# Modulation stage reordered, and one image's group-norm statistics moved into the linear stage

## The reference, cut to what matters

```python
x = x + focal_modulation(_gn(x))     # L0: projection, three depthwise convolutions, modulator, layer norm, projection
x = x + fp8_linear_unit(_gn(x))      # L1: layer norm, 64->512 linear, relu(a)*b, 256->64 linear, both on fp8-rounded values
x = x + gated_scan(_gn(x))           # L2: circular 7x7 convolutions, scan of 8 steps, 64->64 linear
x = x + deform_conv(_gn(x))          # L3: offsets, bilinear gather of 9 taps, linear
def _gn(v, G=32, eps=1e-05):         # mean and variance over all positions and 2 channels
    g = v.reshape(B_, H_, W_, G, C_ // G)
    m = jnp.mean(g, axis=(1, 2, 4), keepdims=True); s = jnp.var(g, axis=(1, 2, 4), keepdims=True)
    return ((g - m) / jnp.sqrt(s + eps)).reshape(v.shape)
```

## Time and profile before

| | |
|---|---|
| median of three runs | 6727.5 us |
| the profiled execution's own time | 6720.4 us |
| its span, first to last instruction | 6718.6 us |
| granted TensorE clock, mean | 0.595 |
| stage C, start to the loads of stage L, groups 0 to 3 | 147.2, 210.3, 211.1, 221.0 us |
| stage L, from there to stage D, groups 0 to 3 | 294, 364, 367, 378 us |

### The profile page before, as it was taken

How to read it: one execution, slowest core, us unless ns; L and a number is a source line. 1 busy time by engine, 2 the same in 40 slices (tenths; PEclk the granted TensorE clock), 3 DMA queues, 4 the chain that set the end, 5 groups by cost and what they waited for, 6 DMA issues and landing times. The chain is left out here.

```text
span 6718.6 us, 66875 instructions
## 1 busy us (share of the span) xinstructions
PE 4037.8 (60%) x26416; PEld 3590.6 (53%) x26416; DVE 3327.1 (50%) x4118; ACT 1743.2 (26%) x3401; POOL 2877.0 (43%) x2617
## 2 busy tenths in 40 slices
PE   5864375678745576579644486667755465365333
PEld 4852275677633575468633385567643365364332
DVE  4357533534578544444478544353468734443332
ACT  2124234311233224321223234321223223022000
POOL 0000002534456544443455543544446645556676
PEclk9955555568555555558555555558655555555555
DMA  2830444458332844448423654439632474843332
GB/s 48 174 53 15 73 115 98 111 131 177 76 84 80 162 130 116 107 107 188 93 77 89 126 134 128 120 88 198 120 91 70 98 161 107 169 128 102 100 94 83
DMA packets 864530, 742.19 MB, mean 110 GB/s; under 512 B 667266, under 2 KB 744482, under 8 KB 860866
## 3 DMA queue, kind: packets, MB, share of 16 engines
q1 hardware_dynamic: 739802, 398.02, 29.9%
q0 software_dynamic: 124416, 339.90, 18.1%
HBM read 621.76 MB, written 117.51 MB: 110 GB/s over the span
## 5 line engine op out<-in xcount | busy, mean ns | idle before, releaser
L2067 POOL DMA_INDIRECT e_gb<-corner_table,e_idx x2592 | 2861.8, 1104 | 3820.5 <-DVE e_vw L2128 1842.4
L2128 DVE TENSOR_TENSOR e_vw<-e_gb,e_pc 128x1024 f32<-128x1024 f32 x576 | 756.4, 1348 | 500.4 <-DMA e_gb<-corner_table,e_idx 260.0
L2081 PE MATMUL e_pw<-wk,e_vt 128*128 128x64 f32 x2304 | 501.6, 391 | 614.8 <-ACT e_vt L2105 284.6
L2081 PEld LDWEIGHTS e_pw<-wk,e_vt 128*128 128x128 f32 x2304 | 471.7, 301 | 667.4 <-ACT e_vt L2105 400.2
L2094 PE MATMUL e_pv<-shifts,e_vw 128*128 128x128 f32 x2304 | 504.0, 392 | 169.4 <-DVE e_vw L2132 109.8
L2094 PEld LDWEIGHTS e_pv<-shifts,e_vw 128*128 128x128 f32 x2304 | 444.8, 222 | 175.1 <-DVE e_vw L2132 112.8
L492 PE MATMUL b_p<-b_x,b_tt 100*100 100x96 f32 x4096 | 423.7, 264 | 42.5 <-issue 42.5
L1467 PE MATMUL d_p<-d_wd,d_px 120*96 120x48 f32 x2048 | 345.4, 355 | 162.1 <-DMA d_px<-x_halo 86.4
L492 PEld LDWEIGHTS b_p<-b_x,b_tt 100*100 100x100 f32 x4096 | 410.4, 181 | 52.8 <-issue 51.7
L1467 PEld LDWEIGHTS d_p<-d_wd,d_px 120*96 120x96 f32 x2048 | 343.3, 258 | 167.7 <-DMA d_px<-x_halo 88.7
L2104 ACT ACTIVATE e_vt<-e_pv 128x512 f32<-128x512 f32 x288 | 171.0, 594 | 872.3 <-PE e_pw L2094 429.5
(11 more groups left out here) (306 smaller groups left out, 7623.5 us busy)
## 6 DMA issues: line engine op xcount, KB each, us to landing
b_tt<-zl SPq DMA_DIRECT2D x256, 234.0 KB
b_tt<-zl SPq DMA_DIRECT2D x128, 390.0 KB
e_gb<-corner_table,e_idx POOLq DMA_INDIRECT x2592
d_px<-x_halo SPq DMA_DIRECT2D x32, 1152.0 KB
corner_table<-f_xn SPq DMA_DIRECT2D x128, 288.0 KB
f_xall<-xpad SPq DMA_DIRECT2D x10, 2400.0 KB
d_wd<-zl SPq DMA_DIRECT2D x10, 1890.0 KB
x_halo<-d_xo SPq DMA_DIRECT2D x128, 144.0 KB
```

The source lines that it names most:

```text
L2067: nc.gpsimd.indirect_dma_start(self.gb[k][:, 4 * q:4 * q + 4, :].rearrange("p a c -> p (a c)"), None, T.table[m], off)\
L2081: nc.tensor.matmul(o, self.vt[:, q, :], T.wk[:, q, :], start=(q == 0), stop=False)
L2128: v.tensor_tensor(dst, self.gb[k][:, 4 * k0:4 * k1, :].rearrange("p (k a) c -> p k a c", a=4), bc(w, [128, k1 - k0, 4, C], 3), ALU.mult).t ...
```

## The change

In stage C the six products of p = 2 take another order, on PE and on DVE: one part of the older image, the three parts of the newer one, then the other two parts of the older one. The older image's scaled results go to a buffer of their own, `c_xm`, and their addition to `c_xs` comes after the newer image's variance. The statistics of the group's last image (image 3) leave stage C, whose groups i = 4 and 5 get shorter, and are taken in stage L: ACT squares after p = 0 of image 2, and the sums, the variance, the root and the scale come at p = 1 of image 2. The planned lengths of both stages change with it.

```diff
@@ class StageC
-    STEPS = [2, 8, 8, 4] + [8, 9, 12, 8] * (NI - 1) + [8, 1, 7, 6] + [6, 2, 1, 1]
+    STEPS = [2, 8, 8, 4] + [8, 9, 12, 8] * (NI - 1) + [8, 2, 7, 1] + [1] * 4
+        self.xm = sb("xm", [PP, NR, C])
...
+    @staticmethod
+    def bank_of(k, second, g):
+        base = 0 if k == 0 else 3 + 6 * (k - 1)
+        if k == NI:
+            return base + g
+        if second:
+            return base if g == 0 else base + 3 + g
+        return base + g + (k > 0)
@@ StageC.pe
-        if k >= 2 and p == 0:
+        if 2 <= k <= NI and p == 0:
             gn.pe_sum_wide(pe, self.psn, gn.use(G, 1, k - 2))
...
         if 1 <= k <= NI and p == 2:
-            for g in range(3):
...
+            back(0)
         if k < NI and p == 2:
             pe.wait_ge(S.c_gwr, NI * G + k + 1)
             for g in range(3):
...
+                forth(g)
+        if 1 <= k <= NI and p == 2:
+            back(1)
+            back(2)
@@ StageC.act
-        if 1 <= k <= NI and p == 3:
+        if 1 <= k < NI and p == 3:
             act.wait_ge(S.c_x1, NI * G + k)
             gn.act_square(act, self.xs[:, (k - 1) % 2, :, :], self.sq[:, :, :], gn.use(G, 1, k - 1))
@@ StageC.dve
+        if old:
+            back(0)
+        if new:
             dve.wait_ge(q_in[u], 80 * G + 16 + 32 * (k // 2 + 1))
...
             link(v.tensor_reduce(s1, self.xo[:, u, :, 0:C], AX.X, ALU.add))
             link(v.tensor_scalar(s1, s1, 1.0 / C, None, ALU.mult))
             link(v.tensor_tensor(s1, s1, s1, ALU.mult))
+        if old:
+            back(1)
+            back(2)
+        if new:
             dve.wait_ge(S.c_sq, NI * G + k + 1)
             link(v.tensor_reduce(s2, self.sq[:, :, :], AX.X, ALU.add))
             link(v.scalar_tensor_tensor(s2, s2, 1.0 / C, s1, ALU.mult, ALU.subtract))
             v.tensor_scalar(s2, s2, 0.0, 1e-3, ALU.max, ALU.add).then_inc(S.c_var, 1)
+        if old:
+            dve.wait_ge(x_in[m % 2], 80 * G + 16 + 32 * (m // 2 + 1))
+            dve.wait_ge(S.c_m_free, 24 * G + self.bank_of(k, True, 2) + 1)
+            v.tensor_tensor(self.xs[:, m % 2, :, :], self.xs[:, m % 2, :, :], self.xm[:, :, :], ALU.add).then_inc(S.c_x1, 1)
+            dve.wait_ge(S.c_x1, NI * G + m + 1)
...
-        if 1 <= k <= NI and p == 3:
+        if 1 <= k < NI and p == 3:
             gn.dve_sums(dve, PP, self.xs[:, (k - 1) % 2, :, :], self.sq[:, :, :], gn.use(G, 1, k - 1))
-        if k == NI + 1 and p == 3:
+        if k == NI and p == 3:
             self.st.leave(dve)
@@ class StageL
-    STEPS = [14, 16] + [14, 7, 10, 10, 10, 9, 8] * (NI - 1) + [14, 8, 6, 10, 10, 8, 12] + [1]
+    STEPS = [14, 16] + [14, 7, 10, 10, 10, 9, 8] * (NI - 2) + [14, 14, 10, 10, 10, 9, 8] + [14, 8, 6, 10, 10, 8, 12] + [1]
@@ StageL.pe
+        if p == 1 and m == NI - 2:
+            gn.pe_sum(pe, self.psn, 128, gn.use(G, 1, NI - 1))
@@ StageL.act
+        if p == 0 and m == NI - 2:
+            self.loaded(act, G, NI - 1)
+            gn.act_square(act, self.xs[:, (NI - 1) % 3, :, :], self.ex[:, :, :], gn.use(G, 1, NI - 1))
...
+        if p == 1 and m == NI - 2:
+            gn.act_std(act, 128, gn.use(G, 1, NI - 1))
@@ StageL.dve
+        if p == 1 and m == NI - 2:
+            i = gn.use(G, 1, NI - 1)
+            self.loaded(dve, G, NI - 1)
+            gn.dve_sums(dve, 128, self.xs[:, (NI - 1) % 3, :, :], self.ex[:, :, :], i)
+            gn.dve_var(dve, link, self.psn, 128, i)
+            gn.dve_scale(dve, link, 128, i, T.norm1[:, NI - 1, :, :])
```

More of the change, by code:

```diff
@@ L894, in pe @@
             self.st.enter(pe, G, 2)
-        m, t2, m2 = k - 1, self.turns(k, True, 6), self.turns(k, True, 3)
-        t1, m1 = self.turns(k, False, 6), self.turns(k, False, 3)
+        m, t2, t1 = k - 1, self.turns(k, True, 6), self.turns(k, False, 6)
         if 1 <= k <= NI and p == 0:
@@ L915, in pe, with back, forth @@
                 last.then_inc(S.c_t_full, 1)
-        if 1 <= k <= NI and p == 2:
-            for g in range(3):
[L918 to L922, removed]
+        def back(g):
+            n = self.bank_of(k, True, g)
+            pe.wait_ge(S.c_t_free, 48 * G + t2 + 2 * g + 2)
+            upto(pe, S.c_m_free, 24 * G + n - 1)
+            for i in range(8):
+                last = nc.tensor.matmul(self.psm[n % 2][:, i, :], self.xt[:, 8 * g + i, :], T.wp[:, :], start=True, stop=True)
+            last.then_inc(S.c_m_full, 1)
+        def forth(g):
+            n = self.bank_of(k, False, g)
+            pe.wait_ge(S.c_t_free, 48 * G + t1 + 2 * g + 2)
+            upto(pe, S.c_m_free, 24 * G + n - 1)
+            for i in range(8):
+                last = nc.tensor.matmul(self.psm[n % 2][:, i, :], self.ct[:, 8 * g + i, :], T.wh[:, k % 2, :], start=True, stop=True)
+            last.then_inc(S.c_m_full, 1)
+        if 1 <= k <= NI and p == 2:
+            back(0)
         if k < NI and p == 2:
@@ L977, in dve, with back @@
             self.st.enter(dve, G, 2)
[L978 to L993, removed]
+        m, u, s1, s2 = k - 1, k % 2, self.s1[:, :], self.s2[:, k % 2, :]
+        old, new = 1 <= k <= NI and p == 2, k < NI and p == 2
+        def back(g):
+            n = self.bank_of(k, True, g)
+            dve.wait_ge(S.c_m_full, 24 * G + n + 1)
+            v.tensor_tensor(self.xm[:, 8 * g:8 * g + 8, :], self.psm[n % 2],
+                            bc(self.rs[:, m % 2, 8 * g:8 * g + 8], [PP, 8, C], 2), ALU.mult).then_inc(S.c_m_free, 1)
+        if old:
+            back(0)
+        if new:
             dve.wait_ge(q_in[u], 80 * G + 16 + 32 * (k // 2 + 1))
             for g in range(3):
-                dve.wait_ge(S.c_m_full, 24 * G + m1 + g + 1)
-                v.tensor_tensor(self.xo[:, u, 8 * g:8 * g + 8, 0:C], self.qs[:, u, 8 * g:8 * g + 8, :], self.psm[(m1 + g) % 2], ALU.mult)\
+                n = self.bank_of(k, False, g)
+                dve.wait_ge(S.c_m_full, 24 * G + n + 1)
+                v.tensor_tensor(self.xo[:, u, 8 * g:8 * g + 8, 0:C], self.qs[:, u, 8 * g:8 * g + 8, :], self.psm[n % 2], ALU.mult)\
                     .then_inc(S.c_m_free, 1)
-            dve.wait_ge(S.c_m_free, 24 * G + m1 + 3)
+            dve.wait_ge(S.c_m_free, 24 * G + self.bank_of(k, False, 2) + 1)
             dve.sem_inc(S.c_xo, 1)
@@ L1011, in dve @@
             v.tensor_tensor(self.xo[:, u, :, C], s2, self.rs[:, u, :], ALU.mult).then_inc(S.c_aug, 1)
-        if 1 <= k <= NI and p == 3:
+        if 1 <= k < NI and p == 3:
             gn.dve_sums(dve, PP, self.xs[:, (k - 1) % 2, :, :], self.sq[:, :, :], gn.use(G, 1, k - 1))
-        if k >= 2 and p == 0:
+        if 2 <= k <= NI and p == 0:
             gn.dve_var(dve, link, self.psn, 128, gn.use(G, 1, k - 2))
-        if k >= 2 and p == 1:
+        if 2 <= k <= NI and p == 1:
             gn.dve_scale(dve, link, 128, gn.use(G, 1, k - 2), T.norm1[:, k - 2, :, :])
-        if k == NI + 1 and p == 3:
+        if k == NI and p == 3:
             self.st.leave(dve)
@@ L1056, in __init__ @@
         self.lin = (S.l_in0, S.l_in1, S.l_in2)
+        self.psn = pb[4][:, 6 * C:8 * C]
         self.sd, self.od = (t.rearrange("b (j p) c -> b p j c", p=128) for t in (T.x1, T.x2))
```

## The result

The changed kernel takes 6773.42 us in the median of seven runs, the kernel before 6731.88 in seven: 1.0059 times as long, 95% interval 1.0041 to 1.0076, that is 28 to 51 us slower (the difference of the medians is 42). In a later comparison, in which the kernel before took 6655.5 us, the same pair gave 1.0057, 1.0035 to 1.0080. The forecast was +51.5 us and 6779.

A forecast was written before the change was run, and what follows sets the result against it. No engine is full, so waits between engines, read stage by stage, bound the kernel. Terms without L's tiles, +2.1, plus +49.4 for those tiles gave +51.5 on 6720.4: 6771.9, with 7.1 for the median 6779; range 6708 to 6798.

The forecast's parts named there:

- The products' order: Stage C, last product to reciprocal root: -0.8 us for group 0's three images, -0.5 for the other nine; -6.9, range -21 to 0.
- The handover: Last store of C to first load of L: gaps fall to 5.3 and 5.7 us; -21.9, range -27 to -10.
- the tiles moved within C: Weighs moved in stage C: +3.6 us in group 3, -1 each in groups 1 and 2; +1.6, ends -4 to +8.
- the handover does not shorten: Rival, C to L: something else holds L's loads, 12 to 22 us of gain go, about 6795; within the forecast's 0.57.
- The statistics in L: Stage L, full DVE: 4 x 7.6 us added, 1.1 saved in group 0's stage D; +29.3, range +19 to +35.
- The tiles in front of the multiplies: Stage L, line 1294: weighs in eight new places behind long gather chains slow the multiplies; +49.4 us, range -5 to +58.
- the bad place: Kernel before, stage L, group 3, image 3: weigh before line 1294, 25 unbroken gathers, multiplies 22.7 us against 14.7; 7.3 lost.
- How long the gathers are: Stage L: gathers beside DVE's quantising are slow, 2285 ns longest against median 949; otherwise nine would be about 9 x 1.3 shorter.
- Its signs: Line 1294 20 to 23 us in five of eight places, C-to-L gap 5 to 6, group 0's root 4.7 after last product.
- the chain breaks: Rival, stage L: gather chain breaks, the eight places cost -5 us in all, 6725, no change; chance 0.22.
- Faster: Rival, stage C: the same loss leaves groups 1 to 3, about 6 us each, -18; with first rival -21, 6706; chance 0.21.
- The change does not do what it says: Rival, stage C: older image's last additions delay `c_aug` equally; first term 0, forecast up 7 to 6786; within the forecast's 0.57.

## Why the prediction was right, step by step

- **The products' order, -6.9:** right in its place and its size in group 0 (4.5 us where 4.7 was forecast), where C falls by 3.1 for three images with the statistics in their old place, 2.4 forecast. Beside tiles the stage times show next to nothing of the other 4.5 (-0.4 in all three groups), while the comparison shows -14 with at least -5. Which is true of groups 1 to 3 stays open.
- **The handover, -21.9, and the tiles moved within C, +1.6:** right in mechanism, and near in size because two errors cancel. Gaps of 5.3 to 6.3 us. At the old places it brings 26.5 (C 773.0 to 746.5; by group 3.1, 6.1, 6.3 and 11.0), where the forecast had 30.9 before anything was given back. Of moved tiles it had 9 given back in group 3, 3.6 more there, and 2 gained in groups 1 and 2, +10.6 in all. Measured in C, group 3 gives back 6.4 and groups 1 and 2 gain 2.6 and 3.8, which is nothing on balance; group 3 pays again in L (below). C as a whole: -29.0 and -30.3, forecast -27.2. The rival "the handover does not shorten" is out. The Trainium skill warns of a long wait until a write is complete ("Perfetto Trace Analysis", section "DMA Instruction — HWDGE (DVE, Sync)"); the traces agree with the 5.3 to 6.3 us that are left.
- **The statistics in L, +29.3:** right. 7.6 us on DVE in group 0, and L is 32.1 longer with them than without at the same places (1442.5 against 1410.4). By group it is 4.8, 8.4, 9.5 and 9.4, where 6.5 and three times 7.6 were forecast: group 0 was put too high and the groups with tiles too low.
- **The tiles in front of the multiplies, +49.4:** right mechanism, mis-sized. L is 27.8 longer at the new places (1470.3 against 1442.5). Two things were off. The chain was taken for given in eight places and broke in three, where POOL had caught up with the weigh and paused for 1.7 us: 8 + 6.9 us. That the weighs stand at the same distances as in the bad place did not decide it. And a slow place costs 5.2 to 5.9 above 14.7 in the changed kernel's first trace, not 6.9. Its chain had 27 gathers (45 in group 3) and reached 7.1 us into the multiplies, the observed one had 36 and reached 9.6, that is 8.7 to its last start; that this is the reason is likely, not shown. The 13.3 us of group 3's image 0, which the prediction used for its lower end, stood at a granted clock of 0.61, the 14.7 beside it at 0.50, so that they are no fair pair. By group the picture is less neat than the sum. Groups 1 and 2 are 7.3 and 6.0 longer, with 9.8 of slow steps in each, so that the moved tiles gave 2 to 4 back elsewhere. Group 3 is 14.3 longer with one new slow place of 4.9: the other 9 stand beside the tile that its L has more, for which the prediction had no term in L, only its 9 for two tiles at the handover.
- **How long the gathers are:** the prediction put nine gathers at 9 x 1.3 us over their usual length. That takes the longest for all: the 25 gathers of the earlier trace rows are 3.9 us over 949 ns each, all taken together.
- **What the sum left out:** the other stages, taken at nothing. They show +28 in one pair of traces and +5 in the other. C and L together give +30 and +29 in the two pairs (-29.0 + 59.0, -30.3 + 59.6), where the forecast was 51.5. Some 8 us of the other 12 of the medians' 42 may be stage D's, where the planner moved tiles too (above); no run changed the places of D alone, and the cause of the rest is open. So the forecast came nearer to the measured time than its terms deserve: it put 20 us too much on C and L and left out D.
- **Its signs:** five of the eight places were to take 20 to 23 us. Three did, and two took 19.9; in the changed kernel's second trace all five are at 19.5 to 19.8. Group 0, C and L together, was to change by +0.4 and did by -0.5 and -1.1.
- **The rivals:** "the chain breaks" came true in three places of eight; the changed code at the old places shows what its time would have been, no change (0.9992). "Faster" needed 6 us from each of groups 1 to 3 in stage C beside the handover; with the products' order alone they gave 2.5, none and -2.0. "The change does not do what it says" is out by group 0's 3.1 us and by the interval of the products' order, which ends at -5.

## What to carry to other kernels

A planner's planned lengths are part of a change: put the new code on the old places, and the old code on the new ones, before judging either. Moving a dependent chain from a gap in which an engine idles into a stage where that engine is full trades one for the other; here 27 us of gap against 32 us in the stage where DVE is full. And a place that is slow once in the trace of before is the best price list for a plan that puts more work into the same place, as long as one checks how it came about (here 27 to 45 gathers without a pause) for each new place.

## What the runs showed of the hardware

The slow steps come in a unit. The starts of line 1328 in the first slow place of the changed kernel, a timeline of DVE:

```profile
1986.35 0.42 DVE L1328 TENSOR_TENSOR l_g<-l_ra,l_p 128x256 f32<-128x256 f32 x1 [3.77 <-issue]
1988.42 0.42 DVE L1328 TENSOR_TENSOR l_g<-l_ra,l_p 128x256 f32<-128x256 f32 x1 [1.65 <-ACT l_ra L1241]
1991.25 0.42 DVE L1328 TENSOR_TENSOR l_g<-l_ra,l_p 128x256 f32<-128x256 f32 x1 [2.41 <-issue]
1994.79 0.42 DVE L1328 TENSOR_TENSOR l_g<-l_ra,l_p 128x256 f32<-128x256 f32 x1 [3.12 <-ACT l_ra L1241]
```

The first steps are 2.07, 2.83 and 3.54 us, then 1.43 (the next start is at 1996.22): about 3, 4, 5 and 2 times 0.71. The same shows on PE in stage C of group 1, a timeline of PE in the changed kernel. One part is eight products, sixteen matmuls in the trace, with no wait between them in the program. The first eleven ran 0.17 us apart; these are the last five:

```profile
1709.40 0.27 PE L939 MATMUL c_p<-wh,c_ct 66*100 66x64 f32 x1 [0.47 <-issue]
1710.80 0.58 PE L939 MATMUL c_p<-wh,c_ct 66*100 66x64 f32 x2 [1.14 <-issue]
1712.23 0.26 PE L939 MATMUL c_p<-wh,c_ct 66*100 66x64 f32 x1 [0.84 <-issue]
1713.62 0.27 PE L939 MATMUL c_p<-wh,c_ct 66*100 66x64 f32 x1 [1.12 <-issue]
```

The four rows start 1.4 us apart, twice the same unit, where matmuls of this line take 0.17 us each elsewhere (8.21 us for 48), and a run of 18 gathers without a pause had its last start at 1710.1. Since nothing in the program holds these matmuls, late semaphores can't be the whole of it; the trace fits engines that get their instructions late behind a long chain of gathers. No run took this apart: it is argued, not shown. Shown is that a pause of some 4 us put into the chain takes the slow steps away, all but 1.1 us, and that nearly the same chain costs 5 us with a weigh 5 us ahead of the handshakes and 0.6 to 1.5 with it 11 us ahead (with 36 gathers 3.4). The changed kernel's own three quick places had a pause of 1.7 us. Why the weigh's place matters is open too.
